# Attention heads in units of four instead of two, with the interleaved work of three images put in another order

## The reference

```python
x = x + scan_layer(group_norm(x))      # in_proj, 3x3 conv + silu, 4 scan paths, norm, gate, out_proj
t = tokens(x)                          # 256 tokens x 192
t = t + attn(ln(t))                    # layer l=0: 12 heads of 16, causal
h = ln(ln(t)); ...                     # layer l=1: 12 heads of 16, not causal
x1 = x + attn(h); x2 = x1 + gelu(x1 @ mlp_w1) @ mlp_w2
out = x2 + sum_e comb[e] * (gelu(ln(x2) @ exp_w1[e]) @ exp_w2[e])   # 4 experts, all computed, top 2 weighted
```

## Time and profile before

| | us |
|---|---|
| median of 3 runs | 899.87 (895.37 to 905.07) |
| the profiled execution, its own time | 906.1 |
| its span, first to last instruction | 904.1 |
| mean granted clock of TensorE (share of 2.4 GHz) | 0.826 |

### The profile page before, as it was taken

One profiled execution on the slowest core, in us unless ns is written; L12 is line 12 of the kernel. 1 busy time (PEld: TensorE's weight loads), 2 busy tenths in 40 slices (PEclk: granted clock), 3 DMA queues, 4 the chain that ended last, 5 costly groups with the idle time before them and its releaser, 6 DMA issues. The chain is left out here.

```text
span 904.1 us, 8598 instructions
## 1 busy us (share of the span) xinstructions
PE 634.5 (70%) x3104; PEld 422.4 (47%) x3104; DVE 570.0 (63%) x931; ACT 306.4 (34%) x571; POOL 215.5 (24%) x184
## 2 busy tenths in 40 slices
PE   1405556583557768885878788967888878887597
PEld 1201114342322347464534565655446656765486
DVE  3559964666689845775699658675998444533210
ACT  0133303122323204256254232555443234343131
POOL 5215540131234410103244201022343110000100
PEclk9999656575678759787899888888889898999789
DMA  6988810035567100048274000364660000000000
GB/s 151 285 189 197 194 39 9 1 36 130 124 139 180 30 9 1 9 65 209 67 178 115 14 5 0 46 169 108 152 162 9 0 1 1 1 1 9 1 1 9
DMA packets 28623, 68.87 MB, mean 76 GB/s; under 512 B 5152, under 2 KB 12976, under 8 KB 28592
## 3 DMA queue, kind: packets, MB, share of 16 engines
q1 hardware_dynamic: 28592, 68.47, 32.6%
HBM read 60.33 MB, written 3.93 MB: 71 GB/s over the span
## 5 line engine op out<-in xcount | busy, mean ns | idle before, releaser
L1536 POOL TENSOR_TENSOR state<-state,C_rows 128x1024 f32<-128x1024 f32 x42 | 113.3, 2697 | 203.1 <-DVE state L1112 203.1
L1112 DVE TENSOR_TENSOR_SCAN state<-decay,dx_rows 128x512 f32<-128x512 f32 x84 | 127.6, 1559 | 12.7 <-PE py L679 8.9
L679 PE MATMUL py<-state,sel 128*96 128x512 f32 x168 | 100.2, 735 | 46.7 <-POOL state L1536 46.6
L1401 ACT ACTIVATE decay<-d_rows,a_neg 128x255 f32<-128x255 f32 x192 | 81.4, 496 | 132.1 <-DMA d_rows<-delta_dram 96.1
L750 PE MATMUL pd<-w_dn,act 128*128 128x192 f32 x480 | 90.5, 343 | 3.7 <-ACT act L1414 3.7
L1105 DVE TENSOR_TENSOR dx_rows<-dx_rows,B_rows 128x1024 f32<-128x1024 f32 x48 | 74.4, 1551 | 21.4 <-DMA dx_rows<-delta_x_dram 21.4
L750 PEld LDWEIGHTS pd<-w_dn,act 128*128 128x128 f32 x480 | 82.7, 200 | 7.1 <-ACT act L1414 4.6
L679 PEld LDWEIGHTS py<-state,sel 128*96 128x96 f32 x168 | 30.8, 197 | 94.7 <-POOL state L1536 57.8
L734 PE MATMUL pu<-fT,w_up 128*128 128x256 f32 x180 | 61.6, 426 | 12.1 <-ACT act L1414 11.7
L532 PE MATMUL ps<-hT,w_qkv 96*96 96x256 f32 x128 | 44.1, 519 | 33.9 <-DVE hT L1255 33.2
L905 PE MATMUL pm<-probs,v_aug 128*32 128x256 f32 (+1 forms) x384 | 52.2, 397 | 13.8 <-DVE inv_den L1314 8.2
(11 more groups left out here) (230 smaller groups left out, 1151.8 us busy)
## 6 DMA issues: line engine op xcount, KB each, us to landing
d_rows<-delta_dram SPq DMA_DIRECT2D x48, 512.0 KB, 6.6
dx_rows<-delta_x_dram SPq DMA_DIRECT2D x48, 512.0 KB, 5.2
w_dn<-exp_w_dram SPq DMA_DIRECT2D x1, 2304.0 KB
B_rows<-xdbl SPq DMA_DIRECT2D x4, 512.0 KB, 7.0
C_rows<-xdbl SPq DMA_DIRECT2D x4, 512.0 KB, 10.8
w_up<-exp_w_dram SPq DMA_DIRECT2D x1, 1536.0 KB
delta_dram<-delta SPq DMA_DIRECT2D x4, 384.0 KB, 3.0
delta_x_dram<-delta_x SPq DMA_DIRECT2D x4, 384.0 KB, 3.4
```

What stands on the lines that cost most here:

```text
L679: mm = nc.tensor.matmul(py[0:INNER, :], sel[:, first:first + INNER], flat(states[g % held])[:, paths], start=False, stop=(g == GROUPS - 1) ...
L1112: ins = nc.vector.tensor_tensor_scan(flat(states[g % held])[:, both], flat(decay[g % 2])[:, both], dx_rows[g % 2][:, both], 0.0, ALU.mult, ...
L1401: ins = nc.scalar.activation(decay[g % 2][:, k, rest], d_rows[g % 2][:, k, rest], ACT.Exp, scale=a_neg[:, at:at + 1])
L1536: nc.gpsimd.tensor_tensor(now, now, C_rows[:, :], ALU.mult).then_inc(sc_done, 1)
```

## The change

- Units of four heads, three per attention. Queries and keys are projected by weights padded on the host so that head j of a unit stands in rows 32j to 32j+15: 6 outputs of 128 channels (float32) instead of 4 of 96. The copies out of PSUM are 3 on ScalarE (q) and 3 on VectorE (k). The high and low parts, `to_stack` and its matmuls and copies are gone.
- Scores and shifted scores are float32 matmuls of 16 (17) rows, four at a time in strips of 32 rows (`tile_position=(32 * j, 0)`), strip j into bank j of `ps`.
- A unit takes all four banks and the one `probs`: `scores(u+1)` waits for the exponentials of u, exponentials wait for `context(u-1)`.
- `context(u)` has four column positions in turn and follows `scores(u+1)`; `spread` and `invert_sums` are placed anew.
- All five tables are new. In the first "output" slot VectorE no longer scans: scans 0 and 1 come in (1, "turned"), behind its copy of hT.
- Weight loads: `w_qk` 590 KB and `w_v` 147 KB per attention instead of `w_qkv` 442 KB.

```diff
 SSM_STEPS = {
-    (0, 1): [("in_proj",)],
-    (0, 2): [("silu",)],
-    (0, 5): [("x_dbl", 0)],
+    (0, 0): [("in_proj",)],
+    (0, 4): [("silu",)],
+    (0, 6): [("x_dbl", 0)],
     (0, 7): [("x_dbl", 1)],
-    (0, 9): [("dt", 0)],
-    (0, "spread"): [("dt", 1), ("softplus", 0), ("softplus", 1), ("softplus_log",)],
-    (1, 9): [("y_copy",)],
-    (1, 10): [("y_norm",)],
-    (1, "context"): [("y_turn",)],
-    (1, "spread"): [("y_out",)],
+    (0, 8): [("dt", 0)],
+    (0, 9): [("dt", 1), ("softplus", 0), ("softplus", 1), ("softplus_log",)],
+    (1, "context"): [("y_copy",)],
+    (1, "spread"): [("y_norm",)],
+    (1, "output"): [("y_turn",), ("y_out",)],
 }
 DECAYS = {
+    (0, "output"): [0, 1],
+    (1, "projected"): [2, 3],
+    (1, 0): [4, 5],
+    (1, 1): [6],
+    (1, 4): [7, 8],
+    (1, 5): [9],
+    (1, 8): [10, 11],
 }
 SCANS = {
-    (0, "output"): [0, 1],
-    (1, "projected"): [2],
-    (1, 0): [3, 4],
...
+    (1, "turned"): [0, 1],
+    (1, 0): [2, 3],
+    (1, 1): [4],
+    (1, 4): [5, 6],
+    (1, 5): [7],
+    (1, 8): [8, 9],
+    (1, 9): [10, 11],
 }
 Y_SUMS = {
+    (1, "projected"): [0],
+    (1, 0): [1],
+    (1, 1): [2],
+    (1, 2): [3],
+    (1, 3): [4],
+    (1, 5): [5],
+    (1, 6): [6],
+    (1, 7): [7],
+    (1, 9): [8],
+    (1, 10): [9],
+    (1, 11): [10],
+    (1, "context"): [11],
 }
 FFN_STEPS = {
-    (0, 0): [("up", 0, 1), ("up", 0, 2)],
-    (0, 1): [("down", 0, 0), ("down", 0, 1)],
-    (0, 3): [("norm", 0)],
...
+    (0, 0): [("up", 0, 1)],
+    (0, 1): [("up", 0, 2)],
+    (0, 2): [("down", 0, 0)],
+    (0, 3): [("down", 0, 1)],
+    (0, 4): [("norm", 0)],
     (0, 5): [("norm", 1)],
     (0, 6): [("turn", 1)],
+    (0, 7): [("up", 1, 0), ("logits",)],
+    (0, 8): [("up", 1, 1)],
+    (0, 9): [("turn_gates",)],
+    (0, 10): [("bias",), ("up", 1, 2)],
+    (0, 11): [("up", 2, 0)],
+    (0, "context"): [("down", 1, 0)],
+    (0, "spread"): [("up", 2, 1), ("down", 1, 1)],
+    (0, "output"): [("up", 2, 2)],
     (1, "turned"): [("add", 1), ("up", 3, 0)],
     (1, "projected"): [("down", 2, 0)],
+    (1, 0): [("down", 2, 1), ("up", 3, 1)],
+    (1, 1): [("up", 3, 2)],
+    (1, 2): [("add", 2)],
+    (1, 3): [("down", 3, 0)],
+    (1, 4): [("up", 4, 0)],
+    (1, 5): [("down", 3, 1)],
+    (1, 6): [("up", 4, 1), ("add", 3)],
+    (1, 7): [("up", 4, 2)],
+    (1, 10): [("down", 4, 0)],
+    (1, 11): [("down", 4, 1)],
+    (1, "context"): [("add", 4)],
 }
```

The order of TensorE around a unit, and of VectorE:

```diff
 scores(0)                              # TensorE
-for u in range(UNITS):
-    if u + 1 < UNITS:
-        scores(u + 1)
-    row_max(u)
-    if u >= 1:
-        context(u - 1)
-    others((l, 2 * u))
-    shifted(u)
-    if u in (2, 4):
-        spread(u // 2 - 1)
-    others((l, 2 * u + 1))
-context(UNITS - 1)
+for u in range(HTILES):
+    row_max(u)
+    shifted(u)
+    others((l, 4 * u))
+    if u >= 1:
+        spread(u - 1)
+    others((l, 4 * u + 1))
+    if u + 1 < HTILES:
+        scores(u + 1)
+    others((l, 4 * u + 2))
+    context(u)
+    others((l, 4 * u + 3))
...
+for u in range(HTILES):                # VectorE
+    shift(u)
+    if u >= 1:
+        context_copy(u - 1)
+    others((l, 4 * u))
+    if u >= 1:
+        invert_sums(u - 1)
+    others((l, 4 * u + 1))
+    if u + 1 < HTILES:
+        row_max(u + 1)
+    others((l, 4 * u + 2))
+    others((l, 4 * u + 3))
```

More of the change, by code:

```diff
@@ L44 @@
 A_LOG_MAX = 80.0
-SLOTS = [(l, s) for l in range(2) for s in ("turned", "projected", *range(2 * UNITS), "context", "spread",
+SLOTS = [(l, s) for l in range(2) for s in ("turned", "projected", *range(HEADS), "context", "spread",
                                             "output")]
@@ L557, in block_of @@
             if opening:
-                states += [buf[:, :, :, :].rearrange("p j t q -> p (j t) q") for buf in probs]
+                states += [probs[:, 2 * b:2 * b + 2, :, :].rearrange("p j t q -> p (j t) q") for b in range(2)]
             held = len(states)
@@ L832, in attention, with masks @@
-                        for u in range(4):
-                            stack(u)
-                        others((l, "projected"))
-                        for u in (4, 5):
-                            stack(u)
+                        others((l, "projected"))
+                        def masks(mask):
+                            for j in range(QUAD):
+                                for i in range(TILES):
+                                    at = TOKENS * i + 128 * i
+                                    mm = nc.tensor.matmul(ps[:, j, at:at + 128], identb[:, :], mask[:, :],
+                                                          start=False, stop=True, skip_group_check=True)
+                            return mm
@@ new lines, in scores @@
+                                pe.wait_ge(k_copied[l], HTILES)
+                            else:
+                                pe.wait_ge(p_done[l], u)
+                            for i in range(TILES):
+                                keys = 128 * (i + 1) if causal else TOKENS
+                                for j in range(QUAD):
+                                    rows = slice(32 * j, 32 * j + HEAD)
+                                    mm = nc.tensor.matmul(ps[:, j, TOKENS * i:TOKENS * i + keys],
+                                                          q_quad[rows, u, 128 * i:128 * (i + 1)],
+                                                          k_quad[rows, u, 0:keys],
@@ L854, in scores @@
                                                           start=(i == 0), stop=not causal,
[L855 removed]
+                                                          tile_position=(32 * j, 0), skip_group_check=True)
                             if causal:
[L857 to L862 removed]
+                                mm = masks(maskq)
@@ L1350, in _ @@
                         dve.wait_ge(w_b, 16 * len(b_loads))
+                    if split_w_up:
+                        for l in range(2):
+                            link(nc.vector.tensor_scalar(b_qk[l][:, 1, :], b_qk[l][:, 1, :], top_one[:, :], None,
+                                                         ALU.add))
                     if run_a:
@@ L1662 @@
     }
+    for l in range(2):
+        host[f"w_qk{l}"] = heads_apart(w_qkv[l][:, 0:2 * WIDTH]).reshape(2, CGROUP, 2, HTILES, 128) \
+            .transpose(1, 0, 2, 3, 4)
+        host[f"b_qk{l}"] = heads_apart(b_qkv[l][0:2 * WIDTH])[0].transpose(2, 0, 1)
+        host[f"w_v{l}"], host[f"b_v{l}"] = w_qkv[l][:, 2 * WIDTH:], b_qkv[l][2 * WIDTH:]
     nc = bacc.Bacc("TRN2", target_bir_lowering=False, num_devices=1)
```

284 lines of the change are left out of this document (81 added, 203 removed).

## The result

The changed kernel takes 962.4 us (median of 4 runs, 960.1 to 964.6), the kernel before 900.9: 1.0687 times as long, 95% interval 1.0621 to 1.0752. The forecast was 895.4, and its range ended at 916. Times in us are medians over all runs of a kernel; the ratios leave out the few runs in a slower state. The profiled execution has a span of 958.3 us against 904.1.

A forecast was written before the change was run, and what follows sets the result against it. Bound: a relay across TensorE, VectorE and ScalarE in fixed program order, VectorE's scans in the way. Opening +1.5, second block -12.5, full blocks 2 x 7.0, fifth -7.5 sum to -4.5 us: 901.6 profiled, 895.4 forecast; range 873 to 916.

The forecast's parts named there:

- The counts: Whole kernel: VectorE near 530 us busy, about 4 more table loads per full block, a unit's score records within 1.1 us.
- rival 3: Scores on TensorE: the four strips don't run together, 103 us more, near 998 us; chance 0.03.
- the exclusive lock: Scans: VectorE and a reading GpSimd block each other at shared SBUF ports; a scan group directly behind another costs 5.6 us.
- l=0 of the walk: Full block, l=0, walked piece by piece in each engine's new order: h_tok comes 10.5 us later than before.
- the two stops: Full block, l=0: TensorE stands 8.8 us before bias for gateT and 5 us at up(0,2) for its gelu.
- 12.7 us: End of l=0 in a full block: bias, up, context(2), down, spread and projection steps follow on TensorE, 12.7 us.
- its l=0 ties: Fifth block, without scans: l=0 takes as long as before.
- The -7.5: Fifth block: ends 7.5 us earlier, since the new relay has three hops where the old had six.
- The rest of l=1: Full block, first maxima of l=1 to the end: 86.7 us against 73.0, +13.7, with waits of 2.0 and 6.0.
- The front: Full block, h_tok to first maxima of l=1: 15.1 us against 32.3, -17.2, but with scan 2 not done.
- Rival 2: Full blocks: single banks plus stops, with work at half clock behind them, 19 us more, 914 us; chance 0.22.

The follow-up runs named there:

- e15: Changed kernel with the feed-forward steps at the end of l=0 back in the slots of the kernel before: 1.053, 954.5 us.
- e16: Changed kernel, units of four heads untouched, with every order edit that helped put together: 1.028, 930.5 us.
- e17: e16 with three state buffers, plus dt(1) and the softplus chain back where the kernel before has them: 1.019, 922.3 us.
- e3: Changed kernel with l=1's feed-forward steps and y_sums 3 to 7 moved behind the shifted scores: 1.086, 980.0 us.
- e11: Changed kernel with three state buffers instead of two (five instead of four in the opening): 1.065, 962.7 us.
- e13: Kernel before with three state buffers alone: 0.993, 899.8 us.
- e8: Kernel before with the front of l=1 ordered as the change has it on all engines: 0.997, 898.8 us.
- e9: Changed kernel with short filler matmuls keeping TensorE at work where it stood idle in full blocks: 1.067, 962.3 us.
- e10: Changed kernel with only l=1's feed-forward steps moved from between scores and turned maxima, y_sums left in place: 1.060, 957.8 us.

## Why the prediction was wrong

**The counts held.** VectorE has 536.3 us (about 530 forecast), table loads rose from 17 to 21 in a full block, 16 score records of a unit take 0.94 us in l=0 and 1.15 in l=1 (1.0 taken), and at most 2.09 at the lower clock where 3.5 was the price of strips one after another, so four float32 strips run together and rival 3 is out; a scan directly behind another took 4.37 us again. GpSimd's product beside it:

```profile
648.49 3.25 POOL L1472 TENSOR_TENSOR state<-state,C_rows 128x1024 f32<-128x1024 f32 x1 [4.23 <-DVE state L1069]
```

It ends at 651.74 (alone such a product takes 2.35 us), and the two scans, whose row runs from 649.56 to 653.93, end 2.2 us behind it, about the 2.34 that they take alone. With that the trace agrees with the exclusive lock of the Trainium skill, SBUF — State Buffer, "Who interferes with whom".

**The step that failed first: l=0 of the walk (+10.5, measured +21.0, or +23.0 by the walk's own marks).** I priced the two stops about right (8.8 us for gateT, measured 7.05; 5 for gelu(0, 1), measured 6.59) and missed what lies behind them on TensorE. Put at this block's start, the walk has scores(1) at 572.7, shift(2) at 597.2 and the end of softplus at 611.4; the trace has 576.7, 605.0 and 621.7. The hop from maxima to shift was walked as if TensorE were free; it was queued behind two `down`, later behind up(1, 0) and the logits. A smaller part is the clock: of the 4.0 us by which scores(1) were late, 2.5 are up(0, 2), scores and masks at the lower clock behind the stop (granted 0.50; 5.5 us, where the unit and the `up` before took 3.0). Behind the last shift the softplus chain on VectorE stood another 3.1 us for dt(0) and 2.8 for the spread, both on TensorE, and h_tok came 12.5 us late. The "12.7 us" of steps between bias and the projection were sized right in this block (622.04 to 634.84); what I did not ask is whether they had to be there. e15 took 6.2 us from the fifth block by moving them, and the edits of e16 and e17 together brought l=0 of the full blocks back to the level of before.

**The same step in the fifth block ("its l=0 ties").** It was argued from the number of hops and not walked. It lost 7.8 us, with maxima 10.6 us earlier. The -7.5 was put on l=1 alone, and there -4.3 came.

**The rest of l=1 (+13.7, measured +21.7).** The waits that the walk lacked are 2.3 us more at shift(1), 2.1 more at shift(2), and 4.15 before scan 3, 8.6 us together. The last was not in the walk at all: with two state buffers a scan waits for the y_sum of two scans before, in TensorE's order. e3, e11 and e13 show that bond from three sides.

**The front (-17.2, measured -15.3)** was right as a mechanism and sized right. Taken as a gain by itself it was wrong in the full blocks: e8 gives the kernel before 9 us of the same front, and 1 us of l=1 is left; in the second block 5.6 of 9.5 are.

**Rival 2** had the sign and its mark: the clock of the full blocks fell under 0.80. Its price was 19 us, a third of the loss. For the most part the clock was the mark of the stops and not the cause: with it back at 0.86 and 0.83 (e9) the blocks are together as long as they were.

**What stays open.** Order alone gave back 4.1 of 6.9 points (e16), with the third buffer and softplus late 5.0; a third buffer also gives the kernel before 0.7. Against the kernel before with three buffers (0.993) the best order found for the changed units is still 2.6 points behind. Part of that is the one order table for all blocks: what helped the full blocks cost the fifth 6.5 us in l=1 (e10). Whether the rest, which lies in the second block and in l=1 of the full ones, is order too, or the units' single set of banks, no run here tells; units of four heads on two sets of banks were not tried.

## What to carry to other kernels

A relay over engines with fixed programs is walked hop by hop with everything that stands ahead of each hop on its engine. Fewer, larger hops on one set of buffers may leave fewer places where other work can hide; that was argued here and not shown by a run of its own. Before a gain in one stretch is added to the sum, ask what paces the stretch behind it (here the return of two buffers): if that is something else, the gain is waited away. When stops come with a low clock, keep the engine busy in them once: if the clock rises and the time stays, the clock was not what cost it.
